# A two-layer perceiver block on one core: cross openings reordered, experts' up products split into fp32r passes

## The chip, the core and the metric

One Trainium2 chip, of which the program uses one core with its engines: TensorE (PE, with its weight loads PEld), VectorE (DVE), ScalarE (ACT), GpSimd (POOL) and the sync engine (SP), which here only issues DMAs. The metric is the time of one execution in device microseconds, lower is better. Before: median 1411.81 us of three runs, 1409.78 to 1412.41.

## The reference

The input x has 16 batches of 64 tokens and 256 features; it is 1024 x 256 as a matrix. Six sublayers each add to x what they compute from its layer norm:

```
x += cross0(norm(x), ctx, mask)          16 heads of 16, 1024 context rows per batch, softmax
x += self0(norm(x))                      attention over the batch axis, rotary, "softmax one"
x += moe(norm(x))                        8 experts, top 2, capacity 256, gelu(rows @ w1) @ w2
x += cross1(norm(x), ctx, bias, mask)    as cross0, with an additive bias row
x += self1(norm(x))                      attention over the sequence, rotary
x += fp4_linear(silu(gate) * up)         weights and activations rounded to a 4-bit grid in blocks of 16
```

For each batch a cross sublayer projects the 1024 x 256 context to keys and values, projects the queries, and forms softmax(q k / 4 + bias) v per head. In the experts, w1 is 256 x 1024 and w2 is 1024 x 256.

## The kernel before

**Cross block.** `cross_block` (line 192 on) runs all 16 batches in one block; batch b has eight steps n, one for each pair of heads. In a step TensorE computes the scores of pair n (`scores`, L476), transposes the probabilities of two steps before (`turn`, L489), and does one piece of the next batch's key or value projection (`project_key`, `project_value`, L419 to L421). In steps 5 and 1 it weighs the values of four pairs (`weigh`, L505). VectorE takes row maxima (L585), inverts the sums (L593), copies half of each transpose (L601) and computes the low part of the keys (`rest_key`, L573). ScalarE does the exponentials (L771), the other half of the copies (L780), the high part of keys (L755), the copies of values (L762) and the high part of the next context (`split_hi`, L747). GpSimd divides (L844), computes the context's low part (`split_lo`, L824) and spreads the queries into a block-diagonal operand (`spread`, L836). Each engine works through its own list in order and waits on semaphores; nothing is reordered at run time.

A projection is exact to fp32 by three fp32r passes: each operand is split into a rounded part hi and a rest lo, and the product is lo·hi + hi·lo + hi·hi:

```
pe.matmul(out, lhs[1], rhs[0], start=first, stop=False)
pe.matmul(out, lhs[0], rhs[1], start=False, stop=False)
return pe.matmul(out, lhs[0], rhs[0], start=False, stop=last)
```

**Opening.** Ahead of the loop over batches lies work for batch 0 and for all queries. TensorE computes batch 0's four key pieces (in the first cross block only the first of them, the other three behind the query products), transposes the first half of the normalized tokens (L520), projects their queries (`project_queries` 0 and 1, L530), computes batch 0's four value pieces, transposes the second half and projects its queries (2 and 3). VectorE splits each query product into hi and lo (`split_queries`, L668 to L672); the sync queue stores them to DRAM (`store_queries`, L336 and L337) and reloads them in the stacked layout (`first_queries`, L343); then `spread` can run, and then the first scores. The sync queue also copies the keys of each pair of heads into their stacked layout, three DMAs a pair (`load_keys`, L329). In the first cross block the queries of group 0 and 1 are stored first and the pairs 0 to 3 follow the reload of group 0, 4 to 7 that of group 1; in the second all eight pairs go ahead of the stores. Queries 2 and 3 are stored last, and ScalarE's first copy of batch 1's values (step 3) waits for those stores, since they lie in the same buffer. GpSimd does batch 1's four `split_lo` before `spread`.

The split of the context of batch b+2 is done in steps 1, 2, 5 and 6 of batch b (`SPLIT_STEPS`), and the load of context b+3 (L311) waits for its last piece, because all contexts come through one raw buffer.

**Experts.** `experts_block` (line 1470 on) does the eight experts one after the other: transposes of the gathered rows (L1516), the up product in eight f tiles of 128 hidden columns (L1530; fp32, two k steps, 256 columns), GELU on ScalarE (L1557), and the down product (L1540). VectorE copies the transposed rows (L1574) and the results (L1587), and in between rounds one chunk of the last sublayer's weights to the 4-bit grid (`Quantizer.run`, L1646 to L1655, ten passes). The sync queue loads up(e) when up product e-2 is done (L1496) and down(e) when down product e-2 is done (L1498). In expert 6 ScalarE and GpSimd also split the second cross block's weights and first context.

## Time and profile before

| what | value |
|---|---|
| median of three runs | 1411.81 us (1409.78 to 1412.41) |
| profiled execution, its own time | 1413.69 us |
| its span | 1411.9 us, 34686 instructions |
| TensorE busy | 1255.7 us (89%) |
| VectorE busy | 963.9 us (68%) |
| ScalarE busy | 760.5 us (54%) |
| GpSimd busy | 642.8 us (46%) |
| granted TensorE clock, mean | 0.926 of full |

Busy time is the time in which an engine works on an instruction; times are in us from the start of the span. The first cross block fills the span up to about 475 us, the experts lie between 626 and 752, the second cross block between 756 and about 1200. In a timeline row the bracket at the end is the idle time ahead of the instruction and what ended it, as far as the semaphores show it; `x4` means four such instructions in a row, merged. A fp32 product appears as two instructions, a fp32r pass as one.

### The profile page before, as it was taken

The numbers are of one execution on the slowest core, as the hardware profiler recorded it, in microseconds if no ns is written. First come the engines' busy times: TensorE is split into PE (matmuls) and PEld (weight loads), VectorE is DVE, ScalarE is ACT, GpSimd is POOL, SyncE is SP. The second block draws the span as 40 slices with busy tenths as digits, with TensorE's granted clock in tenths as the row PEclk, the third lists the DMA queues.
The fourth block names the chain that finished last, engine by engine and source line by source line (L and its number), as shares of the span: only waits on it lengthen the run. The fifth ranks groups of instructions, "written<-read, shape, count | busy, mean of one in ns | idle before, by whom it ended". The sixth has DMA issues, their size and how long they took to land. (4 is left out here: it accounts for less than half of the span.)

```text
span 1411.9 us, 34686 instructions
## 1 busy us (share of the span) xinstructions
PE 1255.7 (89%) x12166; PEld 1050.6 (74%) x12166; DVE 963.9 (68%) x1991; ACT 760.5 (54%) x1379; POOL 642.8 (46%) x580
## 2 busy tenths in 40 slices
PE   5799999999999689549997699999999998677778
PEld 3588888888887548338885588888888887546546
DVE  5477777777777565555515577777777777478896
ACT  2577777777786211102233577777777777124221
POOL 2465666665654314033341566656656654317000
PEclk9899999999999885559999899999999999886899
DMA  6677677777665140244545677777777765100000
GB/s 197 169 181 207 177 188 199 178 193 198 172 170 140 36 60 3 93 152 165 172 158 168 180 202 197 174 194 189 180 195 182 185 167 129 35 0 3 1 4 26
DMA packets 106723, 198.31 MB, mean 140 GB/s; under 512 B 43661, under 2 KB 63790, under 8 KB 106640
## 3 DMA queue, kind: packets, MB, share of 16 engines
q1 hardware_dynamic: 105104, 193.32, 52.0%
q0 software_dynamic: 1536, 3.88, 0.9%
q8 instruction: 53, 0.87, 0.3%
q14 instruction: 30, 0.25, 0.1%
HBM read 88.26 MB, written 10.62 MB: 70 GB/s over the span
## 5 line engine op out<-in xcount | busy, mean ns | idle before, releaser
L844 POOL TENSOR_SCALAR cross_prob<-cross_prob,cross_inverse 128x1024 f32<-128x1024 f32 x256 | 288.7, 1128 | 345.5 <-DVE cross_inverse L593 345.5
L771 ACT ACTIVATE cross_prob<-cross_negated,cross_negmax 128x1024 f32<-128x1024 f32 x256 | 294.9, 1152 | 147.9 <-DVE cross_negmax L585 147.5
L585 DVE CUSTOM_DVE_ANT_0 cross_negated<-cross_scores,cross_bias 128x1024 f32<-128x1024 f32 x256 | 313.5, 1225 | 31.1 <-PE cross_scores L476 13.7
L489 PE MATMUL cross_turn<-ident,cross_prob 128*128 128x128 f32 x2048 | 271.3, 275 | 16.2 <-POOL cross_prob L844 11.9
L489 PEld LDWEIGHTS cross_turn<-ident,cross_prob 128*128 128x128 f32 x2048 | 241.3, 142 | 55.9 <-POOL cross_prob L844 15.8
L780 ACT COPY cross_probT<-cross_turn 128x512 f32<-128x512 f32 x256 | 149.6, 584 | 69.2 <-PE cross_turn L489 68.2
L476 PE MATMUL cross_scores<-cross_keys,cross_qbd 96*128 96x512 f32 x512 | 169.6, 413 | 12.5 <-POOL cross_qbd L836 12.5
L601 DVE COPY cross_probT<-cross_turn 128x512 f32<-128x512 f32 x256 | 175.6, 686 | 5.4 <-PE cross_turn L489 5.4
L824 POOL TENSOR_TENSOR cross_ctx_lo<-cross_raw,cross_ctx_hi 128x512 fp32r<-128x512 f32 x120 | 156.2, 1303 | 25.7 <-ACT cross_ctx_hi L747 25.7
L419 PE MATMUL cross_out<-cross_wv_hi,cross_ctx_lo 128*128 128x256 f32 x488 | 147.4, 302 | 0.0
L421 PE MATMUL cross_out<-cross_wv_hi,cross_ctx_hi 128*128 128x256 f32 x488 | 137.4, 282 | 0.0
L420 PE MATMUL cross_out<-cross_wv_lo,cross_ctx_hi 128*128 128x256 f32 x488 | 137.2, 281 | 0.0
L593 DVE RECIPROCAL cross_inverse<-cross_total 128x1 f32<-128x1 f32 x256 | 41.9, 164 | 131.1 <-ACT cross_prob L771 129.9
L505 PE MATMUL cross_out<-cross_probT,cross_value 128*32 128x128 f32 x4096 | 127.2, 277 | 2.6 <-ACT cross_probT L780 1.8
L505 PEld LDWEIGHTS cross_out<-cross_probT,cross_value 128*32 128x32 f32 x4096 | 109.3, 111 | 26.0 <-issue 24.4
L419 PE MATMUL cross_proj<-cross_ctx_hi,cross_wk_lo 128*128 128x512 f32 x244 | 107.9, 442 | 0.0
L476 PEld LDWEIGHTS cross_scores<-cross_keys,cross_qbd 96*128 96x128 f32 x512 | 83.9, 191 | 32.2 <-POOL cross_qbd L836 14.1
L420 PE MATMUL cross_proj<-cross_ctx_lo,cross_wk_hi 128*128 128x512 f32 x244 | 97.5, 399 | 0.0
L421 PE MATMUL cross_proj<-cross_ctx_hi,cross_wk_hi 128*128 128x512 f32 x244 | 97.4, 399 | 0.0
L420 PEld LDWEIGHTS cross_out<-cross_wv_lo,cross_ctx_hi 128*128 128x128 f32 x488 | 92.8, 190 | 0.0
L573 DVE SCALAR_TENSOR_TENSOR cross_key_lo<-cross_proj,cross_bk,cross_key_hi 128x512 fp32r<-128x512 f32 x122 | 90.5, 742 | 3.3 <-ACT cross_key_hi L755 3.3
L419 PEld LDWEIGHTS cross_out<-cross_wv_hi,cross_ctx_lo 128*128 128x128 f32 x488 | 92.6, 190 | 0.0
(270 smaller groups left out, 2021.8 us busy)
## 6 DMA issues: line engine op xcount, KB each, us to landing
cross_keys<-cross_key_hi SPq DMA_DIRECT2D x512, 128.0 KB, 2.3
cross_raw<-in_ctxT SPq DMA_DIRECT2D x32, 1024.0 KB, 5.6
cross_keys<-cross_key_lo SPq DMA_DIRECT2D x256, 128.0 KB, 2.4
cross_bias<-bias_rows SPq DMA_DIRECT2D x32, 512.0 KB, 3.6
up_sb<-in_moe_w SPq DMA_DIRECT2D x8, 1024.0 KB, 9.1
down_sb<-in_moe_w SPq DMA_DIRECT2D x8, 1024.0 KB, 11.2
cross_stacked_q<-q_rows SPq DMA_DIRECT2D x90, 64.0 KB, 2.0
q_rows<-cross_negated SPq DMA_DIRECT2D x8, 256.0 KB, 2.5
```

The lines of the kernel that those rows point to most:

```text
L419: pe.matmul(out, lhs[1], rhs[0], start=first, stop=False)
L420: pe.matmul(out, lhs[0], rhs[1], start=False, stop=False)
L421: return pe.matmul(out, lhs[0], rhs[0], start=False, stop=last)
L476: last = pe.matmul(ps_s[n % 2][:, at], qbd[par][:, n, :, :].rearrange("p h q -> p (h q)"), keys[:, n, at], start=True, stop=True)
L489: last = pe.transpose(ps_t[part][:, k * P:(k + 1) * P], prob[n % 2][:, kt * P:(kt + 1) * P], ident)
L505: last = pe.matmul(ps_o[32 * j:32 * j + 32, 0:P], value[par][:, kt, g * P + 32 * j:g * P + 32 * j + 32], probT[:, j, kt, :], start=(kt == ...
L585: dve.tensor_tensor_reduce(negated[n % 2], ps_s[n % 2][:, :], bias_sb[par][:, :], -1.0, 3.0e38, ALU.add, ALU.min, negmax[:, n % 2:n % 2 + ...
L601: dve.tensor_copy(probT[:, j, 4:8, :], ps_t[1][:, :].rearrange("p (k q) -> p k q", k=4)).then_inc(turn_copied_v, 1)
L771: act.activation(prob[n % 2][:, :], negated[n % 2], ACT.Exp, bias=negmax[:, n % 2:n % 2 + 1], scale=-1.0, accum_out=total[:, n % 2:n % 2 + ...
L780: act.copy(probT[:, j, 0:4, :], ps_t[0][:, :].rearrange("p (k q) -> p k q", k=4)).then_inc(turn_copied_a, 1)
L824: pool.tensor_tensor(ctx_lo[par][:, :, at], raw[:, :, at], ctx_hi[par][:, :, at].bitcast(F32), ALU.subtract).then_inc(lo_done, 1)
L844: pool.tensor_scalar(prob[n % 2][:, :], prob[n % 2][:, :], inverse[:, n % 2:n % 2 + 1], 1.0, ALU.mult, ALU.mult).then_inc(prob_ready, 1)
```

## The change

**Cross openings.** On the sync queue keys and queries are interleaved: two pairs ahead in the first cross block (`taken is None`) and three in the second, then store of group 0, a pair, reload of group 0, store of group 1, a pair, reload of group 1. After the second context and batch 1's queries come the other pairs, with the stores of queries 2 and 3 between them, and the load of the output weights last. TensorE does all four key pieces ahead of the tokens in both blocks, and the query products 2 and 3 move into steps 0 and 1 of batch 0, behind the scores. Their splits on VectorE move to the same steps and get buffers of their own. In the second block VectorE's key rests and query splits move ahead of some of the additions of the experts' results. ScalarE splits context 1 ahead of the value copies. GpSimd, in the second block, spreads group 0 between the two halves of its context split. In batch 0 the context splits move from steps 1, 2, 5, 6 to 3, 4, 6, 7.

**Experts.** The up product uses three fp32r passes. ScalarE rounds the weights (four pieces) and the rows to their high part and takes over the copies of the results; VectorE computes the low parts. `up_hi`, `up_lo`, `rows_hi` and `rows_lo` are single buffers; the load of up(e) now waits only until the low part of expert e-2 is there. The norm's buffers are freed before the experts to make room. The weights' 4-bit rounding uses the class `Rounding` of the last sublayer: eight passes, of which the last comes behind the low parts. `Rounding` computes with negated scales; the sign of the silu input goes with it.

```diff
@@ cross_block, sync @@
-            def first_keys(g):
-                sp.wait_ge(key_lo_done, 2 * g + 2)
-                for n in range(4 * g, 4 * g + 4):
-                    load_keys(n)
+            def first_keys(n):
+                if n % 4 == 0:
+                    sp.wait_ge(key_lo_done, n // 2 + 2)
+                load_keys(n)
...
-            if taken is not None:
-                for g in range(G):
-                    first_keys(g)
-            for g in range(G):
-                store_queries(g, first_q_stored[g])
-            for g in range(G):
-                first_queries(g)
-                if taken is None:
-                    first_keys(g)
+            ahead = 2 if taken is None else 3
+            for n in range(ahead):
+                first_keys(n)
+            store_queries(0, first_q_stored[0])
+            first_keys(ahead)
+            first_queries(0)
+            store_queries(1, first_q_stored[1])
+            first_keys(ahead + 1)
+            first_queries(1)
             sp.wait_ge(lo_done, 8)
             load_ctx(2)
-            first.load_out(sp)
             sp.wait_ge(qbd_ready, G)
             load_queries(1)
-            for n in range(G, len(q_jobs)):
-                store_queries(n, q_stored)
+            for n in range(ahead + 2, 6):
+                first_keys(n)
+            store_queries(2, q_stored)
+            first_keys(6)
+            store_queries(3, q_stored)
+            first_keys(7)
+            first.load_out(sp)
@@ TensorE: four key pieces first; in body @@
                     scores(b, par, n)
+                    if is_first(b) and n < G:
+                        project_queries(G + n)
@@ VectorE, second block @@
-                for i in range(5, NT):
-                    through(i)
-                    rest_key(0, 0, i - 5)
-                shift(1)
-                rest_key(0, 0, 3)
-                for n in range(G):
-                    split_queries(n)
+                through(4)
+                through(5)
+                rest_key(0, 0, 2)
+                split_queries(0)
+                rest_key(0, 0, 3)
+                through(6)
+                through(7)
+                shift(1)
+                split_queries(1)
@@ ScalarE @@
+            copy_tokens(0)
+            for piece in range(4):
+                split_hi(1, 1, piece)
             for piece in range(4):
                 copy_value(0, 0, piece)
             copy_tokens(1)
-            for piece in range(4):
-                split_hi(1, 1, piece)
@@ GpSimd, second block @@
+                for piece in range(2):
+                    split_lo(1, 1, piece)
+                spread(0, 0, 0)
+                for piece in range(2, 4):
+                    split_lo(1, 1, piece)
+            spread(0, 0, 1)
@@ all @@
+        def split_steps(b):
+            return (3, 4, 6, 7) if is_first(b) else SPLIT_STEPS
@@ experts_block, sync @@
-                sp.wait_ge(hidden_ready, FT * (e - 1))
+                sp.wait_ge(up_divided, PIECES * (e - 1))
@@ TensorE @@
+                    pe.wait_ge(up_divided, PIECES * e + f * PIECES // FT + 1)
                     for g in range(G):
-                        last = pe.matmul(ps_h[f % 3][:, :], up[par][:, g, f * P:(f + 1) * P], rowsT[par][:, g, :],
-                                         start=(g == 0), stop=(g == G - 1))
+                        hi, lo = (part[:, g, f * P:(f + 1) * P] for part in (up_hi, up_lo))
+                        pe.matmul(ps_h[f % 3][:, :], lo, rows_hi[:, g, :], start=(g == 0), stop=False)
+                        pe.matmul(ps_h[f % 3][:, :], hi, rows_lo[:, g, :], start=False, stop=False)
+                        last = pe.matmul(ps_h[f % 3][:, :], hi, rows_hi[:, g, :], start=False, stop=(g == G - 1))
@@ ScalarE @@
+                if e + 1 < E:
+                    round_up(e + 1)
+                    round_rows(e + 1)
                 if e == E - 2:
                     first.round_weights(act)
+                for half in range(CT):
+                    copy_result(e, half)
+                if e == E - 2:
                     first.round_context(act)
@@ VectorE @@
+                    fp4.scale_and_round(dve, c, e)
                 if e + 1 < E:
-                    copy_turn(e + 1)
+                    rest_of_up(e + 1)
+                    rest_of_rows(e + 1)
```

`round_up(e)` is four ScalarE copies of 512 elements per partition into `up_hi`, `rest_of_up(e)` four VectorE subtractions into `up_lo`; `round_rows` and `rest_of_rows` do the same for the transposed rows in PSUM.

## Rows read from the trace of the kernel before

**Rows 1.** Windows, all engines: stretch, length, busy us, granted clock, DMA share.

```profile
70.00:460.00 390.00, 386.80 (x4160) 339.86 (x4154) 295.66 (x595) 298.79 (x528) 232.16 (x203) 1.00 0.71 181
58.50:64.00 5.50, 5.44 (x18) 4.58 (x19) 2.37 (x6) 4.46 (x8) 3.28 (x4) 0.50 0.17 65
628.20:638.20 10.00, 9.96 (x32) 8.25 (x33) 9.48 (x10) 2.69 (x7) 9.68 (x10) 0.69 0.11 28
645.58:652.49 6.91, 6.91 (x34) 6.03 (x33) 6.40 (x11) 2.69 (x7) 4.47 (x4) 1.00 0.61 205
```

**Rows 2.** Timeline, TensorE, opening of the first cross block: start, length, instruction.

```profile
37.52 1.03 PE L520 MATMUL cross_turn<-ident,cross_probT 128*128 128x128 f32 x8
...
46.50 1.49 PE L476 MATMUL cross_scores<-cross_keys,cross_qbd 96*128 96x512 f32 x4 [3.47 <-POOL cross_qbd L836]
...
58.56 1.94 PE L489 MATMUL cross_turn<-ident,cross_prob 128*128 128x128 f32 x8 [3.44 <-ACT cross_probT L780]
...
71.03 0.73 PE L476 MATMUL cross_scores<-cross_keys,cross_qbd 96*128 96x512 f32 x2
```

**Rows 3.** Timeline of the same opening, GpSimd and ScalarE.

```profile
39.87 5.58 POOL L824 TENSOR_TENSOR cross_ctx_lo<-cross_raw,cross_ctx_hi 128x512 fp32r<-128x512 f32 x4 [16.54 <-ACT cross_ctx_hi L747]
45.41 2.03 POOL L836 TENSOR_TENSOR cross_qbd<-cross_stacked_q,half_mask 96x512 fp32r<-96x512 f32 x2
...
56.74 0.62 ACT L747 CAST cross_ctx_hi<-cross_raw 128x512 fp32r<-128x512 f32 x1 [3.47 <-DMA cross_raw<-in_ctxT]
...
60.72 0.59 ACT L762 COPY cross_value<-cross_out 128x512 f32<-128x512 f32 x1 [0.66 <-DMA q_rows<-cross_value]
```

**Rows 4.** Timeline, TensorE, opening of the second cross block.

```profile
765.99 3.70 PE L530 MATMUL cross_scores<-cross_probT,cross_wq 128*128 128x512 f32 x8 [0.81 <-ACT cross_probT L787]
...
775.93 1.32 PE L520 MATMUL cross_turn<-ident,cross_probT 128*128 128x128 f32 x8 [0.51 <-DVE cross_probT L661]
...
790.64 2.07 PE L476 MATMUL cross_scores<-cross_keys,cross_qbd 96*128 96x512 f32 x4 [9.01 <-POOL cross_qbd L836]
...
809.61 0.73 PE L476 MATMUL cross_scores<-cross_keys,cross_qbd 96*128 96x512 f32 x2
```

**Rows 5.** Timeline of the same opening, sync queue, GpSimd and VectorE.

```profile
768.39 0.55 SPq L329 DMA_DIRECT2D cross_keys<-cross_key_hi  x1
...
770.95 1.01 POOL L851 TENSOR_TENSOR cross_rstd<-cross_shifted,cross_power 128x4 f32<-128x4 f32 x1 [7.69 <-DVE cross_shifted L655]
...
771.44 0.74 DVE L668 TENSOR_SCALAR cross_prob<-cross_scores,cross_bq 128x512 f32<-128x512 f32 x1
...
773.40 0.75 DVE L668 TENSOR_SCALAR cross_prob<-cross_scores,cross_bq 128x512 f32<-128x512 f32 x1
...
783.60 0.58 SPq L336 DMA_DIRECT2D q_rows<-cross_negated  x1
...
786.81 2.74 SPq L343 DMA_DIRECT2D cross_stacked_q<-q_rows  x6
...
789.55 1.04 POOL L836 TENSOR_TENSOR cross_qbd<-cross_stacked_q,half_mask 96x512 fp32r<-96x512 f32 x1 [5.50 <-DMA cross_stacked_q<-q_rows]
```

**Rows 6.** Timeline, TensorE, value products of the first opening, first and last of 48.

```profile
31.77 0.28 PE L419 MATMUL cross_scores<-cross_wv_hi,cross_ctx_lo 128*128 128x256 f32 x1
...
37.40 0.28 PE L421 MATMUL cross_out<-cross_wv_hi,cross_ctx_hi 128*128 128x256 f32 x1
```

**Rows 7.** Timeline, ScalarE and TensorE, second batch of the second cross block.

```profile
822.07 0.62 ACT L747 CAST cross_ctx_hi<-cross_raw 128x512 fp32r<-128x512 f32 x1 [0.16 <-DMA cross_raw<-in_ctxT]
...
823.98 0.59 ACT L780 COPY cross_probT<-cross_turn 128x512 f32<-128x512 f32 x1 [0.70 <-PE cross_turn L489]
...
826.04 1.04 PE L489 MATMUL cross_turn<-ident,cross_prob 128*128 128x128 f32 x8
```

**Rows 8.** DMA issues: tensors, engine, count, KB each, median us to landing.

```profile
down_sb<-in_moe_w SPq DMA_DIRECT2D x8, 1024.0 KB, 11.2
...
q_rows<-cross_value SPq DMA_DIRECT2D x8, 256.0 KB, 4.7
```

More of the change, by code:

```diff
@@ L549, in _ @@
             turn_tokens(1)
-            for n in range(G, 2 * G):
-                project_queries(n)
             def body(b, par):
@@ L686, in _ @@
             shift(0)
-            through(4)
+            if start is not None:
+                through(4)
+            else:
+                dve.wait_ge(rows_loaded, 48)
+                dve.wait_ge(q_loaded, 32)
+                rest_key(0, 0, 0)
+                rest_key(0, 0, 1)
             normalize(0)
@@ L694, in _ @@
                 dve.wait_ge(q_loaded, 32)
-                rest_key(0, 0, 0)
+                for piece in range(4):
+                    rest_key(0, 0, piece)
                 dve.wait_ge(rows_stored, 32)
@@ L1553, in _, with round_up, round_rows, copy_result @@
         def _(act):
+            def round_up(e):
+                if e >= 2:
+                    act.wait_ge(up_loaded[e % 2], 16 * (e // 2))
+                for p in range(PIECES):
+                    act.copy(up_hi[:, :, piece_of(p)], up[e % 2][:, :, piece_of(p)]).then_inc(up_rounded, 1)
+            def round_rows(e):
+                act.wait_ge(turned, e + 1)
+                act.copy(rows_hi[:, :, :], ps_t[:, :, :]).then_inc(rows_rounded, 1)
+            def copy_result(e, half):
+                act.wait_ge(result_ready, 2 * e + half + 1)
+                if half == 0 and e >= 2:
+                    act.wait_ge(scattered[e - 2], 16 * CT)
+                act.copy(result[e % 2][:, half, :], ps_y[half][:, :]).then_inc(result_copied, 1)
+            round_up(0)
+            round_rows(0)
             for e in range(E):
@@ L1744, in multiply, with __init__, part, scale_and_round @@
         return eng.tensor_tensor(self.by_block(out), self.by_block(self.v[:, at]), self.wide(self.scale, self.blocks_of(at)), ALU.mult)
+class GatedWeights:
+    ROWS = 2 * GU // P
+    TAILS = [(c, min(P, GU - c * P)) for c in range(-(-GU // P))]
+    ROW_CHUNKS = [(0, 3), (3, 6), (6, 9), (9, ROWS)]
+    def __init__(self, sb, gate_upT, downT):
+        self.gate_up, self.down = sb("gate_up_sb", [P, self.ROWS, D]), sb("down_sb", [P, G, GU])
+        self.gate_upT, self.downT = gate_upT, downT
+        self.q = Rounding(sb, "fp4w", 3 * D)
+        self.step, self.total = sb("fp4w_step", [P, 3 * D]), sb("fp4w_total", [P, 3 * D])
+    def part(self, chunk):
+        if chunk < len(self.ROW_CHUNKS):
+            first, end = self.ROW_CHUNKS[chunk]
+            return self.gate_up[:, first:end, :].rearrange("p r d -> p (r d)")
+        return self.down[:, chunk - len(self.ROW_CHUNKS), :]
+    def scale_and_round(self, dve, c, chunk):
+        x = self.part(chunk)
+        at = slice(0, x.shape[-1])
+        c.link(self.q.scales(dve, c, x, at))
+        c.link(self.q.divide(dve, x, at))
+        c.add(self.q.round(dve, c, self.step, self.total, at))
+    def multiply(self, dve, chunk):
+        x = self.part(chunk)
+        return self.q.multiply(dve, x, slice(0, x.shape[-1]))
+    def turn_row(self, pe, r, ps, ident):
+        for g in range(G):
+            last = pe.transpose(ps[:, g * P:(g + 1) * P], self.gate_up[:, r, g * P:(g + 1) * P], ident)
+        return last
+    def copy_row(self, act, r, ps):
+        return act.copy(self.gate_upT[:, :, r * P:(r + 1) * P], ps[:, :].rearrange("p (g n) -> p g n", g=G))
+    def turn_tail(self, pe, c, ps, ident):
+        m = self.TAILS[c][1]
+        for g in range(G):
+            last = pe.transpose(ps[0:m, g * P:(g + 1) * P], self.down[:, g, c * P:c * P + m], ident)
+        return last
+    def copy_tail(self, act, c, ps):
+        m = self.TAILS[c][1]
+        return act.copy(self.downT[0:m, c, :], ps[0:m, :])
 class Ahead:
```

171 lines of the change are left out of this document (56 added, 115 removed).

## The prediction

> **What bounds the kernel now.** I read the stretches first. In the middle of a cross block TensorE is busy for 386.8 of 390.0 us at granted clock 1.00, and in an expert's up stage for 6.91 of 6.91 us [rows 1]. So time is bought in two ways only: fewer TensorE cycles in the experts, or removing the idle time at the two openings, where TensorE has nothing. The timeline of the openings shows that idle time. In opening 1 the last token transposes end at 38.5, four query products follow, and the first scores start at 46.50, held by the spreading on GpSimd [rows 2]. GpSimd had spread late because four context subtractions of 5.58 us stand before the spreading, and they started at 39.87 [rows 3]. Two ScalarE waits follow, for the third context (56.74, 3.47 us) and for the stored queries (60.72, 0.66 us) [rows 3], and TensorE stands still for 3.44 us and goes on at 0.50 of its clock [rows 1, 2]. In opening 2 the first scores wait until 790.64, 9.01 us idle [rows 4]: all 24 key transfers are issued first (768.39 on), the queries are stored only at 783.60 and reloaded at 786.81, and the spreading starts at 789.55 [rows 5]. In the experts TensorE never waits, so every us of product there is one of the end.
>
> **Part 1, the experts' up products.** Each expert had 32 fp32 instructions of 256 columns in 6.91 us [rows 1], 0.216 each. Now there are 8 x 2 x 3 = 48 fp32r passes of the same shape, 128 x 128 weights and 256 columns. The opening's value products are exactly that: 48 passes from 31.77 to 37.40, (37.40 - 31.77) / 47 = 0.120 apart [rows 6]. 48 x 0.120 = 5.75, so 1.16 us less; experts 1 to 7 give 8.1. Bounds: 0.107 a pass if only the columns count (half of the 0.216 that a two-fold fp32 instruction takes), 12.1 us in all; above, 0.190, about the length of a weight load (6.03 us by 33 loads is 0.183) [rows 1], under the rivals. I take 0.120, the same form.
> The Trainium skill, "TensorE: Matmul & The Clock Gate", Part 3, says that a weight load overlaps a running matmul only when the row group differs. By it load and stream would add to about 0.30 a pass and the experts would become some 60 us slower; rows 6 speak against it, since 0.120 is below one load.
> Expert 0's up product filled 628.2 to 638.2 at a mean clock of 0.69 [rows 1]; between the levels 0.50 and 1.00 that is half speed for 0.31 / 0.50 x 10 = 6.2 us, until 634.4. Its token rows now go through a ScalarE cast and then a VectorE subtraction instead of one copy: about 0.74 more (a 512-element VectorE pass of rows 5), start 629.0. At half the clock an f tile of 6 passes takes 6 x 0.213 = 1.28 (twice the column time), so 4.2 tiles until 634.4, then 3.8 x 0.72 = 2.7: end at 637.1 against 638.2, gain 1.1.
> The work around it: ScalarE gets four casts (about 0.62 each [rows 7]), one row cast and two result copies per expert, VectorE four subtractions and one (3.7). They start when the last f tile is done and run under the down product, 6.9 us long by the same instruction count. The chain of casts and subtractions needs about 0.5 + 4 x 0.62 + 0.7 + 0.74 = 4.4 of 7.3, so 2.9 us of cover remain. VectorE's fp4 rounding has two passes fewer and its last multiply stands behind the subtractions: hidden. One place isn't: in expert 6 the order on ScalarE is weights, two result copies, context casts, and the second result is ready only at the end of the down product. The context casts (four, 2.2 us with their overlap) then stand ahead of expert 7's first GELU by 1.8 us, and with three banks TensorE stalls for about 1.0 (0 if they hide, 2.2 if nothing does). The loads: down(e) and then up(e+1) are now issued together, at the end of a down product; a down load takes 11.2 us to landing [rows 8], an up load is of the same size, so both are there after 11.2 to 22.4. The first cast of up(e+1) is due after 5.75 + 0.43 + 6.9 + 5.75 + 0.5 = 19.3, with 2.9 of cover: 0.2 us late at the very worst, which I cost at 0. The Trainium skill, "DMA: Bandwidth & Descriptors", gives about 2 us and bytes over 436 GB/s, an estimate of 4.4 us for 1 MB, also no wait; the row here is more than twice that.
> Sum of part 1: 8.1 + 1.1 - 1.0 = 8.2.
>
> **Part 2, opening 1.** TensorE now does all key products before the tokens. Piece 0 starts at 14.4, pieces 1 to 3 wait for the fourth context subtraction (17.9); with passes of 512 columns at 0.43 (four times 0.107) at half speed, and about 0.23 once the clock has risen, which I put at 21.8, they end at 23.9 (0.43 throughout: 25.6). Tokens 1.0, copies 1.1, two query products 3.7 (the same instructions as in [rows 4]): end 29.7. This is 2 us later than before, and two VectorE splits of 1.96 each [rows 5] end at 31.85. Store, reload and spread then take what opening 2 shows: two stores issued in 1.0, the reload at most 2.1 behind them, three reload issues 1.4, landing 1.4 behind [rows 5]. The interleaved transfer of pair 2 (1.9) fills the wait for the store. Group 0: store 29.9, pair 2 until 32.8, reload until 34.3, landed 35.7, spread until 36.8. ScalarE's four casts come now directly behind the first token copies (26.0 to 28.2), and GpSimd's 5.58 us end at 32.3, so they no longer stand in the way. TensorE's value products (5.75 from 29.7) and second transposes end at 36.7. First scores at 36.8 against 46.50: 9.7 earlier. What is late next is the ScalarE copy of the next batch's first value in step 3. It waits for the second queries' stores, which the sync queue issues behind: reload of group 1 (until 38.7), context 2, the wait for the second spreading (41.1), the next queries (1.6), pairs 4 and 5 (3.8), one store, pair 6 (1.9), the other store. That is 50.2, landed 52.0. ScalarE would be there at 47.8: a wait of 4.2 us, so the exponential of step 3 starts at 53.2 (61.7 before). From there: turn 2 at 53, scores 5 at 56, product of group 0 at 59.5, scores of step 6 at 61.4 against 71.03 [rows 2], gain 9.6. The added query products (1.9 each) in steps 0 and 1 and their splits are in these times; before, they stood ahead of the loop in TensorE's idle time.
> Two costs: the clock may fall in the new wait, as it did behind 3.44 us of idle time [rows 2]; half speed costs an instruction its own time again, I take 0.9 (0 to 2.7, half of the 5.5 us stretch of rows 1). And the split of context 2 ends in step 7 instead of 6, so context 3 is fetched 2.9 us later. In the second cross block that cast had waited 0.16 for its transfer, and the transpose two steps on stood at 826.04 with its copy started at 823.98 [rows 7]; 2.9 late with about 2.2 of slack costs 0.7 (0 to 2.9).
> Part 2: 9.6 - 0.9 - 0.7 = 8.0.
>
> **Part 3, opening 2.** TensorE's order stays, VectorE's changes: the first two key rests at 762.0, so that pairs 0 to 2 leave at 763.5 (5.7 us of issues; eight pairs took 15.2 from 768.39 to 783.60 [rows 5]), group 0 is split at 769.9 and stored, pair 3, reload at 773.0, landed 776.5 at latest. GpSimd's second root now ends at 774.7 (3 us later than the row, since two additions moved behind the split), two context subtractions 2.8: 777.5, spread until 778.5. The transposes of rows 4 end at 777.3, so the scores start at 778.6 against 790.64: 12.0 earlier. The second group: split 775.5, reload until 780.2, spread 783.3; then as in part 2 to the last store, issued until 790.4, landed 792.3. ScalarE would be there at 789.2; wait 3.5. Exponential of step 3 at 793.9, 8.2 later the scores of step 6: 802.1 against 809.61 [rows 4], 7.5. Less 0.5 for the clock and 0.7 for context 3: 6.3.
>
> The other edits (silu without a scale, the buffers' places, the output weights' load moved behind the keys) move no instruction that anything waits for: 0.
> **Sum:** 8.2 + 8.0 + 6.3 = 22.5. The profiled execution took 1413.69 for a span of 1411.9; 1413.7 - 22.5 = 1391.2 there. It lay 1.9 above the median of 1411.81, so the forecast is 1411.8 - 22.5 = 1389.3 us. Against a change of 0.2% (2.8 us), what a measurement of this kernel can tell from none, this is large.
>
> **Rivals.**
> A, the stores become the gate of both openings. A store of second queries took 4.7 us to landing [rows 8], and here context 2's 1 MB is in the queues with it. 2.5 to 4 us later in each opening, with the half clock for longer: 1389.3 + 7 = 1396. For it: the 0.66 us of rows 3, where this wait already showed. Against: in opening 2 the reload followed a store within 2.1.
> B, the new wait is covered: ScalarE runs ahead of TensorE, and if stores land before ScalarE comes, 3 us of each opening and the half clock come back, 1389.3 - 7 = 1382. For it: pairs issued early free the queues. Against: the count of 14 issues ahead of the last store.
> C, slower: the up passes are paced by the weight load, 0.190, because each pass changes weights and the per-tile waits stop the pulling ahead. 48 x 0.190 = 9.12, 2.2 more than before, 17.7 for eight experts. 1411.8 + 17.7 - 14.3 = 1415.2. It decides from 0.181 a pass on, where an up stage costs 6.91 + 14.3 / 8 = 8.7. Against it stand rows 6.
> D, the openings don't gain at all, since later work catches up on the same transfers: 1411.8 - 8.2 = 1403.6. Against: TensorE is busy for 99% afterwards [rows 1], so an earlier start can't be absorbed.
>
> **Chances.** Forecast 0.68, A 0.14, B 0.11, D 0.04, C 0.03. The range: the likeliest one's unknown costs (clock 0 to 2.7, context 3 0 to 2.9, expert 7 0 to 2.2) give 1385 to 1394; with most of A and B 1382 to 1397. Faster by over 0.2%: 0.96; within 0.2%: 0.02; slower: 0.02 (C's time lies just over 0.2%).
>
> **What would show it.** Up products in 5.75 us with 48 passes 0.120 apart; TensorE idle of about 1 us in expert 7's up stage behind a GELU; first scores 9.7 and 12.0 us earlier, counted from the block's start; a ScalarE wait for the query stores of 3.5 to 4.2 us in step 3 of both first batches; a wait for the context in step 1 of the second batch near 3 us. The prediction is wrong if passes are over 0.15 apart, if the scores wait for spreading beyond 40, or if a load of expert weights appears as a wait.

## The result, and the profile after

Changed kernel: median 1399.93 us of 8 runs (1398.30 to 1403.66); kernel before, on the same chip: 1411.01 of 8 (1407.66 to 1414.08). The ratio is 0.9925, 95% interval 0.9913 to 0.9938: faster by 11.1 us. The forecast was 22.5 us faster, and its range ended at 1397. In the profiled executions the span went from 1411.9 to 1399.4, 12.5 us. Cut at points that both traces have, this is where the time went (us; a minus is time gained):

| stretch | before | after | change | forecast |
|---|---|---|---|---|
| start to first weighing of values, cross 1 | 69.15 | 62.77 | -6.4 | -8.7 |
| first to fifth weighing | 52.40 | 54.40 | +2.0 | +0.7 |
| fifth weighing to routing table | 495.07 | 494.99 | -0.1 | 0 |
| routing table to experts' first turn | 9.73 | 13.14 | +3.4 | 0 |
| first turn to cross 2's first key product | 130.34 | 120.96 | -9.4 | -8.2 |
| first key product to first weighing, cross 2 | 51.04 | 46.17 | -4.9 | -7.0 |
| first to fifth weighing | 52.38 | 54.21 | +1.8 | +0.7 |
| fifth weighing to the end | 551.79 | 552.76 | +1.0 | 0 |

Opening 1, TensorE's timeline (start, duration, engine and line, operation, out<-in; in brackets the idle time ahead and its releaser). L483 are scores, L496 turns, L512 the weighing. The two score rows answer to [rows 2].

```profile
37.84 0.74 PE L483 MATMUL cross_scores<-cross_keys,cross_qbd 96*128 96x512 f32 x2 [1.70 <-POOL cross_qbd L837]
...
56.02 1.89 PE L496 MATMUL cross_turn<-ident,cross_prob 128*128 128x128 f32 x8 [4.48 <-ACT cross_probT L785]
...
64.65 0.73 PE L483 MATMUL cross_scores<-cross_keys,cross_qbd 96*128 96x512 f32 x2
```

The scores start 8.7 us earlier than before, but only 6.4 are left at step 6 (71.03 in [rows 2]): TensorE stood still for 4.48 us, as predicted in place and longer in size, and its granted clock was 0.51 from 56.0 to 59.4. Who held it shows in ScalarE's timeline and the sync queue's: the last of the four store issues (two halves for each group), and the copy that waits for them.

```profile
54.80 0.58 ACT L767 COPY cross_value<-cross_out 128x512 f32<-128x512 f32 x1 [5.42 <-DMA q_rows<-cross_value]
...
79.57 0.62 ACT L752 CAST cross_ctx_hi<-cross_raw 128x512 fp32r<-128x512 f32 x1 [2.62 <-DMA cross_raw<-in_ctxT]
...
107.02 0.62 ACT L752 CAST cross_ctx_hi<-cross_raw 128x512 fp32r<-128x512 f32 x1 [2.95 <-DMA cross_raw<-in_ctxT]
```
```profile
39.61 0.43 SPq L314 DMA_DIRECT2D cross_raw<-in_ctxT  x1
...
47.73 0.58 SPq L339 DMA_DIRECT2D q_rows<-cross_value  x1
...
51.35 0.44 SPq L340 DMA_DIRECT2D q_rows<-cross_value  x1
...
73.74 0.39 SPq L314 DMA_DIRECT2D cross_raw<-in_ctxT  x1
```

The store issued until 51.8 was there at 54.8, 3.0 us later. The waits for a context at 79.57 and at 107.02 are the 2.0 us between the first and the fifth weighing; the forecast had only the first of them.

The experts' start, TensorE (L1530 turns, L1544 to L1546 the three passes) and GpSimd's and the sync queue's issues:

```profile
625.30 1.11 PE L1530 MATMUL experts_t<-ident,experts_rows 128*128 128x128 f32 x4 [9.54 <-DMA experts_rows<-stored_rows,gather_at]
...
627.82 0.58 PE L1544 MATMUL experts_h<-experts_rows_hi,experts_up_lo 128*128 128x256 f32 x1 [1.40 <-DVE experts_rows_lo L1621]
...
643.38 0.28 PE L1545 MATMUL experts_h<-experts_rows_lo,experts_up_hi 128*128 128x256 f32 x1
...
648.89 0.28 PE L1546 MATMUL experts_h<-experts_rows_hi,experts_up_hi 128*128 128x256 f32 x1
```
```profile
617.54 1.66 POOL L1643 DMA_INDIRECT experts_rows<-stored_rows,gather_at  x1 [30.24 <-POOLq L1357]
...
619.51 1.25 POOL L1643 DMA_INDIRECT experts_rows<-stored_rows,gather_at  x1 [0.30 <-issue]
```
```profile
619.96 0.37 SPq L1510 DMA_DIRECT2D up_sb<-in_moe_w  x1
```

Expert 1's passes from 643.38 to 648.89 are the second to the last of 48: 5.51 / 46 = 0.120 apart, the forecast's pace. But the first turn stands idle for 9.54 us ahead of it; in the kernel before it was 6.12 (626.35). Expert 2's 1 MB of up weights is now issued at 619.96, in the middle of the gathers; before it left at 638.43. The second gather, issued at 619.51, landed at 625.26.

Opening 2, VectorE's timeline (L670 to L674 split the second group, L663 normalizes the second half) and TensorE's:

```profile
765.70 1.74 DVE L674 TENSOR_TENSOR cross_negated<-cross_prob,cross_negated 128x512 fp32r<-128x512 f32 x1
767.47 5.36 DVE L663 TENSOR_SCALAR cross_probT<-x,cross_moments,cross_rstd 128x256 f32<-128x256 f32 x4
```
```profile
746.26 0.77 PE L426 MATMUL cross_scores<-cross_ctx_hi,cross_wk_lo 128*128 128x512 f32 x1 [3.25 <-PEq L2057]
...
756.62 3.70 PE L537 MATMUL cross_scores<-cross_probT,cross_wq 128*128 128x512 f32 x8 [0.87 <-ACT cross_probT L792]
...
768.85 0.41 PE L527 MATMUL cross_turn<-ident,cross_probT 128*128 128x128 f32 x2 [2.79 <-DVE cross_probT L663]
...
772.25 1.54 PE L527 MATMUL cross_turn<-ident,cross_probT 128*128 128x128 f32 x6 [2.98 <-DVE cross_probT L663]
...
773.44 1.20 PE L483 MATMUL cross_scores<-cross_keys,cross_qbd 96*128 96x512 f32 x2
```
```profile
765.62 2.93 POOL L825 TENSOR_TENSOR cross_ctx_lo<-cross_raw,cross_ctx_hi 128x512 fp32r<-128x512 f32 x2
768.52 1.08 POOL L837 TENSOR_TENSOR cross_qbd<-cross_stacked_q,half_mask 96x512 fp32r<-96x512 f32 x1
769.56 2.48 POOL L825 TENSOR_TENSOR cross_ctx_lo<-cross_raw,cross_ctx_hi 128x512 fp32r<-128x512 f32 x2
```

Four normalizations took 5.36 us. The same four took 1.38 in the first half of this opening and in the kernel before. One by one they took 1.23, 3.56, 0.40 and 0.40: the first beside a context subtraction, the second (768.63 to 772.19) while GpSimd went through the spreading and two subtractions, the last two with GpSimd idle. TensorE waited twice for the tokens. So the scores came 27.2 us behind the block's first key product instead of the forecast's 22.1 (778.6 less 756.5), which is 6.8 earlier than in the kernel before (33.95) and not 12.0.

One more us went ahead of that. The query products (756.62) start 10.4 us behind the first key product; in the kernel before it was 9.3 (765.99 in [rows 4] less 756.69). The granted clock was 0.50 for the first 6.1 us of the key products, against 3.9 before.

### The profile page after: what moved, and what is told of

The parts are those of the page before. It is cut to its first block and busy times, and to the rows that moved or that the text cites. A ratio compares the mean times of both kernels' runs of the same rounds, so it can differ in the third digit from the quotient of the medians.

```text
span 1399.4 us, 35051 instructions
## 1 busy us (share of the span) xinstructions
PE 1249.0 (89%) x12294; PEld 1050.5 (75%) x12294; DVE 974.2 (70%) x1995; ACT 784.7 (56%) x1435; POOL 636.1 (45%) x580
## 5 line engine op out<-in xcount | busy, mean ns | idle before, releaser
L496 PE MATMUL cross_turn<-ident,cross_prob 128*128 128x128 f32 x2048 | 273.0, 276 | 16.3 <-POOL cross_prob L845 8.9
L496 PEld LDWEIGHTS cross_turn<-ident,cross_prob 128*128 128x128 f32 x2048 | 241.7, 142 | 57.2 <-POOL cross_prob L845 13.0
L483 PE MATMUL cross_scores<-cross_keys,cross_qbd 96*128 96x512 f32 x512 | 170.4, 414 | 1.7 <-POOL cross_qbd L837 1.7
L825 POOL TENSOR_TENSOR cross_ctx_lo<-cross_raw,cross_ctx_hi 128x512 fp32r<-128x512 f32 x120 | 155.8, 1300 | 10.2 <-ACT cross_ctx_hi L752 10.2
L512 PE MATMUL cross_out<-cross_probT,cross_value 128*32 128x128 f32 x4096 | 128.3, 278 | 1.6 <-ACT cross_probT L785 1.2
L512 PEld LDWEIGHTS cross_out<-cross_probT,cross_value 128*32 128x32 f32 x4096 | 110.4, 112 | 25.1 <-issue 23.9
L483 PEld LDWEIGHTS cross_scores<-cross_keys,cross_qbd 96*128 96x128 f32 x512 | 83.4, 190 | 21.0 <-issue 13.8
L428 PEld LDWEIGHTS cross_out<-cross_wv_hi,cross_ctx_hi 128*128 128x128 f32 x488 | 92.9, 190 | 0.0
```

Source lines behind the costliest of these rows:

```text
L483: last = pe.matmul(ps_s[n % 2][:, at], qbd[par][:, n, :, :].rearrange("p h q -> p (h q)"), keys[:, n, at], start=True, stop=True)
L496: last = pe.transpose(ps_t[part][:, k * P:(k + 1) * P], prob[n % 2][:, kt * P:(kt + 1) * P], ident)
L512: last = pe.matmul(ps_o[32 * j:32 * j + 32, 0:P], value[par][:, kt, g * P + 32 * j:g * P + 32 * j + 32], probT[:, j, kt, :], start=(kt == ...
L825: pool.tensor_tensor(ctx_lo[par][:, :, at], raw[:, :, at], ctx_hi[par][:, :, at].bitcast(F32), ALU.subtract).then_inc(lo_done, 1)
```

## The experiments

Each is compared with runs of the kernel before on the same chip (medians 1410.2 to 1410.6). There is no number 7. The intervals reach 2 to 3 us to either side, so besides the ratio I read each trace by the stretches of the table above. Each kernel has one trace, and the same code differs from trace to trace: opening 1 by 2.2 us (the changed kernel and experiment 3), and in the kernels with the change the stretch from the fifth weighing to the routing table from 493.8 to 497.0 and the one from the fifth weighing of cross 2 to the end from 550.1 to 553.2. "Opening 1" is the time of the first weighing, "contexts" the stretch from the first to the fifth weighing (52.4 in the kernel before), "opening 2" first key product to first weighing.

```
kernel                       median   ratio to before, 95%    opening1 contexts table-turn experts opening2 contexts
before                                                         69.2     52.4      9.7      130.3   51.0     52.4
changed                     1399.93  0.9925 [.9913,.9938]      62.8     54.4     13.1      121.0   46.2     54.2
1 experts alone             1405.96  0.9962 [.9947,.9977]      68.9     52.4     13.2      120.6   51.8     52.4
2 openings alone            1406.45  0.9966 [.9950,.9982]      63.7     54.7      9.7      130.3   46.9     53.4
3 up load late              1398.30  0.9917 [.9897,.9938]      65.0     54.8     10.4      120.6   45.9     53.6
4 subtractions behind norm  1401.51  0.9932 [.9911,.9953]      63.3     54.6     13.2      120.4   48.6     53.9
5 split steps as before     1395.52  0.9891 [.9874,.9908]      64.7     52.4     13.1      119.9   46.0     52.4
6 stores ahead              1395.15  0.9895 [.9879,.9912]      59.5     53.5     13.0      120.4   45.7     53.8
8 own home                  1393.95  0.9883 [.9864,.9901]      58.5     53.8     13.0      121.1   45.7     53.8
9 all mends                 1386.07  0.9826 [.9811,.9842]      58.2     53.7     10.4      120.1   42.0     52.4
10 all but 4's              1386.37  0.9843 [.9821,.9865]      57.0     52.4     10.4      120.6   45.9     52.4
11 all, steps as before     1383.93  0.9810 [.9793,.9827]      59.1     52.4     10.4      120.7   42.3     52.4
12 all, and behind queries  1382.59  0.9808 [.9792,.9823]      56.4     52.4     10.5      120.0   42.3     52.4
```

**1 and 2, the two parts alone.** The kernel before with the hunks of the experts, and with those of the cross block.

> The kernel before with the change to the experts alone. The changed kernel's trace gives the expert stage 130.2 -> 120.8 us, a gain of 9.4, and a loss of 3.4 at the first gathered rows, because the load of expert 2's up weights (1 MB) is now issued beside the gathers. Theory 1 (the loss belongs to the experts part): the span falls by 9.4 - 3.4 - 0.5 for the clock = 5.5, about 1405.5 us, and the first turn of the experts comes about 3.4 later behind the routing table than before. Theory 2 (the loss comes from the openings' earlier clock or transfers): 9.4, about 1401.6, and the first turn stands 6.1 us of idle time behind the table, as before. The prediction on record said 8.2: 1402.8.

> The kernel before with the change to the two openings alone, the experts in fp32. From the changed kernel's trace: lead of 4.6 us at the end of the first cross block, 4.9 from opening 2, 1.8 lost again at the third context of opening 2, 0.5 at the last turns: 7.2, about 1403.8 us. Theory 1 (the parts add up): 1403 to 1405, and the first gathered rows are there 6.1 us behind the table. Theory 2 (the parts disturb one another, as by the clock): opening 2 gains the 6.3 that were predicted and the sum is 10 or more, 1401 or less.

The ratios stand for 5.4 and 4.8 us, together 10.2, where the changed kernel's stands for 10.6; the spans fell by 4.8 and 7.2, together 12.0 of 12.5. Within their intervals the parts add up. The later gathered rows belong to the experts' part: 13.2 us behind the table with it, 9.7 without. Opening 2 gained 4.2 us with the cross part alone (51.0 to 46.9), so what it falls short of is its own; theory 2 there is wrong. The median of experiment 2 (1406.45) lies outside theory 1's 1403 to 1405; its profiled span fits (1411.9 less 7.2 is 1404.7).

**3, the load that met the gathers.**

```
+            sp.wait_ge(turned, 1)
             for e in range(2, E):
```

> The changed kernel, but the load of expert 2's up weights waits for the first turn of the experts (one wait more on the sync queue; it is due about 20 us later). Theory 1 (the 1 MB load holds up the gathered rows): the idle time ahead of the first turn falls from 9.5 to about 6.8 us and the end comes 2.7 earlier, about 1397.2. Of the 3.4 us, 0.7 stay, since the first two gathers take 1.66 and 1.25 us to issue instead of 1.21 and 0.96, beside VectorE's subtractions. Theory 2 (the longer issue is the whole cause, and the landing only follows it): no change within 0.5 us, 1399.9. If later loads of weights become late, it is slower: a wait on PE or ACT in expert 2 would show it.

TensorE's first turn in that kernel:

```profile
624.53 1.11 PE L1531 MATMUL experts_t<-ident,experts_rows 128*128 128x128 f32 x4 [6.81 <-DMA experts_rows<-stored_rows,gather_at]
```

6.81 us of idle time, as theory 1 has it to the tenth, and no wait in expert 2 (the experts' stretch stays at 120.6). The two issues still took 1.66 and 1.25 us, which leaves the other 0.7. The medians (1398.30 against 1399.93) don't show it, since the intervals overlap; this opening 1 happened to be 2.2 us longer.

**4, GpSimd's subtractions behind the normalization in opening 2.**

```
             else:
-                for piece in range(2):
+                spread(0, 0, 0)
+                pool.wait_ge(normed, NT)
+                for piece in range(4):
                     split_lo(1, 1, piece)
-                spread(0, 0, 0)
-                for piece in range(2, 4):
-                    split_lo(1, 1, piece)
-            spread(0, 0, 1)
+                spread(0, 0, 1)
```

> The changed kernel with GpSimd in another order in opening 2: spreading of group 0, then a wait until VectorE has normalized the second half, then the four context subtractions, then the spreading of group 1. (In opening 1 both spreadings stand behind the subtractions, as before in effect.) In the changed kernel's trace the four normalizations took 5.36 us beside the subtractions and 1.38 us in the kernel before, and TensorE stood still for 2.79 and 2.98 us in its last transposes. Theory 1 (the two engines hold each other up): they take 1.38 us again, the first scores come 3.5 to 4 us earlier, and the end by 3 to 4 us, about 1396.4. Theory 2 (they were slow for another reason, as their source in memory): still above 4 us and no gain, 1399.9. Rival of theory 1: the later subtractions hold the spreading of group 1 and the third context, and under 1 us is left.

Both the theory and its rival came true, in turn. VectorE, TensorE and ScalarE of that kernel:

```profile
766.90 2.19 DVE L663 TENSOR_SCALAR cross_probT<-x,cross_moments,cross_rstd 128x256 f32<-128x256 f32 x4
```
```profile
769.33 1.00 PE L483 MATMUL cross_scores<-cross_keys,cross_qbd 96*128 96x512 f32 x2
...
788.01 1.94 PE L496 MATMUL cross_turn<-ident,cross_prob 128*128 128x128 f32 x8 [3.75 <-ACT cross_probT L785]
```
```profile
786.80 0.59 ACT L767 COPY cross_value<-cross_out 128x512 f32<-128x512 f32 x1 [4.70 <-DMA q_rows<-cross_value]
```

The normalization takes 2.19 us (its first instruction, beside the spreading, took 1.22, the others 0.40 each), and the scores start 22.3 us behind the first key product, 4.9 earlier. All of it is lost at the next gate: group 1 is spread only behind the subtractions, the sync queue waits for that, the last store leaves at 782.9 and is there at 786.8. The first weighing is 2.4 us later than in the changed kernel.

**5, the split's steps.** `return SPLIT_STEPS` in place of the first batch's (3, 4, 6, 7).

> The changed kernel with one constant put back: in the first batch the context's split stands in steps 1, 2, 5, 6 again instead of 3, 4, 6, 7. Theory 1 (the late last piece holds the next context's load, and that its own cast two and three groups later): context 3 is fetched 2.7 us earlier, the ScalarE waits for a context in the second and third batch (2.6 and 2.9 us in the first block, 3.7 in the second) fall under 0.5, and the interval from the first to the fifth weighing of values falls from 54.4 to 52.4 us in the first block and from 54.2 to 52.4 in the second: 3.8 us in all, about 1396. Theory 2 (context 3 waits for the queues, not for its issue): the waits stay within 1 us of what they were and the time at 1399.9. A loss is possible in the first batch, where the cast of step 1 can wait for context 2; in the changed kernel the stored queries end that wait later anyway.

Theory 1: the contexts' stretches are 52.4 in both blocks, 3.8 us less than in the changed kernel, and the median is 4.4 lower. The profiled execution was the slowest of the four (1400.56): its opening 1 is 1.9 us and its stretch up to the routing table 2.0 us longer than in the changed kernel's trace. The cast in step 1 cost nothing that shows, since ScalarE waits for the stores afterwards (4.32 us there).

**6 and 8, the stores.** In 6 stores 2 and 3 are issued ahead of key pairs 4 to 7 in opening 1. In 8 the second queries' halves lie elsewhere, so that no copy waits for their store:

```
-q_home = [..., first.value1[:, :, :].rearrange("p t d -> p (t d)")]
+q_home = [..., oT[:, :, :].rearrange("p g t -> p (g t)")]
...
-                if isinstance(b, int) and b == 1 and piece == 0:
-                    act.wait_ge(q_stored, 32 * (len(q_jobs) - G))
```

> The changed kernel with another order on the sync queue: the third and the fourth store of queries stand ahead of key pairs 4 to 7 (in opening 2 pair 5 stays between them). In opening 1 the last store then leaves at about 47.7 instead of 51.8. Theory 1 (the ScalarE wait of 5.4 us in step 3 is set by the order of issue): it falls by 4 to about 1.5 us and the first weighing comes 4 us earlier, about 1396. Theory 2 (it is set by how long a store takes beside the 1 MB of context 2, as 4.4 us in opening 2 of the experiment before): the wait ends at 51.5 to 52.5 and 2 to 3 us are gained, about 1397.5. No change at all would mean that another wait stood behind it.

> The changed kernel with the second queries' halves in another buffer (oT, free at that time), so that ScalarE's copy of the next batch's values needs no stored queries; the wait moves to VectorE's first result, in step 6. Theory 1 (this wait is the whole of what opening 1 fell short): the wait of 5.4 us is gone, TensorE doesn't stand still for 4.5 us and keeps its clock, and the first weighing comes 5 to 6 us earlier in opening 1 and 0.5 in opening 2: about 1394. Theory 2 (a wait for the context, 1 MB, takes its place in the same step, since its cast stands two places behind): a wait for DMA of 1 to 4 us at the cast in step 3, and 2 us gained, about 1398.

In 6 the wait is down to 0.50 us and the first weighing comes at 59.5, 3.3 earlier. In 8, theory 1, it comes at 58.5, though its first scores were 1.5 later (39.32 against 37.84). From the first scores to the first weighing it is 19.1 us instead of 24.9, so the wait and the half clock behind it were 5.8 of opening 1. The granted clock stayed at 1.00 there (52.8 to 57.0). ScalarE passes the place of the wait without one, and TensorE stays busy:

```profile
51.22 0.56 ACT L767 COPY cross_value<-cross_out 128x512 f32<-128x512 f32 x1
```
```profile
52.85 0.63 PE L483 MATMUL cross_scores<-cross_keys,cross_qbd 96*128 96x512 f32 x2
53.32 1.04 PE L496 MATMUL cross_turn<-ident,cross_prob 128*128 128x128 f32 x8
```

**9, all mends; 10, the same without experiment 4's order.** (9 has the split in steps 2, 3, 5, 6.)

> All mends together: the queries' own home, the load of expert 2's up weights behind the first turn, GpSimd's subtractions of opening 2 behind the normalization, the context's split of the first batch in steps 2, 3, 5, 6. By the ledger: 2.7 (gathers) + 5.5 (opening 1) + 4 (opening 2, where the earlier scores can now count) + 3.8 (contexts) = 16, about 1384. If the openings end at a context transfer instead, half of 9.5 is left: 1388 to 1390. Not below the changed kernel by 6 or more: the ledger is wrong.

> The kernel with all mends, but GpSimd's order in opening 2 as in the changed kernel (two context subtractions, spreading, two more, spreading), so beside the normalization. Theory 1 (VectorE and GpSimd hold each other up, and this counts once the stored queries no longer gate the opening): the four normalizations take 5.4 us again instead of 2.20, TensorE's idle time in the last transposes goes from 0.92 + 0.64 back to 2.8 + 3.0, and the time from the block's first key product to the first weighing of values in opening 2 grows from 41.95 to about 45.5: about 1389.5. Theory 2 (the 3.7 us between the two kernels at that place came from the context's split steps or the own home): under 1 us, 1386 to 1387.

9 is 13.9 us below the changed kernel's median, 16 expected. 10 shows that experiment 4's order was right, with the gate behind it gone: opening 2 is 42.0 us with it and 45.9 without, and the normalization takes 5.36 us again. The medians of the two (1386.07, 1386.37) don't show these 3.9 us: opening 1 came 1.3 later and the contexts took 1.4 more in 9's profile, both at the same code, and such differences between traces are as large as the effect.

**11 and 12.** 11 is 9 with the split in steps 1, 2, 5, 6. In 12 GpSimd waits in opening 1 for `q_step` 3 ahead of its subtractions.

> The kernel with all mends and the context's split of the first batch in steps 1, 2, 5, 6 instead of 2, 3, 5, 6. In the kernel with all mends a wait of 1.4 us for context 3 and one of 2.8 us for context 4 are left in the first cross block. Theory 1 (they stem from the shifted first pieces): both fall under 0.5 and 1 us comes back, 1385. Theory 2 (they stem from the transfer's own time behind an issue that the last piece, step 6 in both, fixes): they stay, and the early cast in step 1 waits for context 2 on ScalarE: 0 to 2 us slower, 1386 to 1388.

> The kernel with all mends, and in opening 1 GpSimd's four context subtractions wait until VectorE has split the first group of queries. There VectorE's last step took 1.67 us beside them and takes 0.69 alone. Theory 1 (the two hold each other up, and the first scores hang on this split): that step takes 0.69 us, the first query store leaves about 1.0 earlier behind the query product, and the first weighing comes 0.5 to 1.0 earlier: about 1385.3. Theory 2: the second group's split and the normalization are held up in its place (2.1 and up to 5.4 us instead of 1.38), and the second transposes come later than the spreading: slower by 1 to 3 us, about 1388.

11: no wait for a context above 0.9 us is left, and both stretches are as in the kernel before. Theory 1 holds for the wait for context 3 only: it is 1.4 us in 9, 1.6 in 10 and 1.4 in 12, all with steps 2, 3, 5, 6, and gone in 11. The 2.8 us for context 4 are in 9 alone (0.7 in 10, 0.6 in 12), so the steps didn't make them. And 10 and 12 have 52.4 us in both stretches as well: the shifted steps cost no time that these traces show, and the intervals of 9 and 11 overlap. 12, theory 1 on VectorE's row:

```profile
30.07 0.69 DVE L674 TENSOR_TENSOR cross_negated<-cross_prob,cross_negated 128x512 fp32r<-128x512 f32 x1
...
32.51 1.67 DVE L674 TENSOR_TENSOR cross_negated<-cross_prob,cross_negated 128x512 fp32r<-128x512 f32 x1
```

The step takes 0.69 us alone, and the second group's has the 1.67 in its place. The first store of queries is issued 2.0 us after the split begins, and 3.0 in 9, 10 and the changed kernel. From there to the first weighing little of it is left: the weighing comes 27.6 us after the split begins, against 28.0 in 10 and 30.1 in 9, which have the same code in this opening. The 0.4 us against 10 are less than the two traces of the same code differ by, so theory 1's gain isn't shown beyond the store. The median of 1382.59 us is the lowest here, 27.6 below the kernel before; its interval overlaps with 11's.

## Why the prediction was wrong

The mechanisms named were there; the sum failed by 10.0 us of span. Five terms were too good: the gathers by 3.4, opening 1 by 2.3, opening 2 by 2.1, the contexts by 2.4 and the end by 1.0. The experts gave 1.2 more than forecast.

**Part 1, right in size, with a missed place.** "Both are there after 11.2 to 22.4 ... which I cost at 0" looked at whom the loads serve and not at whom they meet. The load of expert 2 was moved by the new wait (`up_divided` of expert 0, done at 619.9) to the gathers of the first rows: 3.4 us lost, of which experiment 3 gives 2.7 back. In the openings the prediction followed each DMA of a moved step, and here it didn't. The other 0.7: the gathers' issue takes 1.66 and 1.25 us beside VectorE's subtractions of the up weights, 1.21 and 0.96 without them (experiment 2). The stage itself went as worked out: first turn to last down product 111.65 to 103.20, 8.4 against 8.2 (13.09 a period instead of 14.25; expert 7's stall 0.68 instead of 1.0). Another 0.9 came behind the last down product, where I had looked for nothing: luck.

**Part 2, the store.** The step "that is 50.2, landed 52.0" was 51.8 and 54.8. The landing of 1.8 had no row of its own; the row of 4.7 us [rows 8] stood in rival A. Here the store ran beside key pairs (context 2 had landed at 45.0, before the first of these stores was issued at 47.73) and took 3.0. The first scores were 1.0 late, and with the half clock the first weighing came at 62.8 instead of 60.4: 2.3 us. The 1.0 is the failure of part 3 in another place. "GpSimd's 5.58 us end at 32.3, so they no longer stand in the way" put them beside VectorE's split of group 0. It began on time (27.91) and took 3.0 us instead of 1.96, its last step 1.67 instead of 0.69, and the store left at 30.94 instead of 29.9. Of rival A (1396, 0.14) the mechanism was there in opening 1, by 1.2 us of landing and not by its 2.5 to 4. In opening 2 the four halves landed 2.1 to 2.7 us behind their issue, and there it was not. Experiments 6 and 8 show that the wait for the stores was the gate of opening 1.

**Part 3, two engines side by side.** "two context subtractions 2.8: 777.5 ... The transposes of rows 4 end at 777.3" put GpSimd's work beside VectorE's as if it were free. It made the normalization 5.36 us and the split 1.74. Nothing of this was in the sum, though the kernel before has it: a split that takes 0.69 alone took 1.63 beside GpSimd's subtractions. That cost 3.9 (9 against 10; 0.4 of it is the clock at the key products, below), of which some was hidden in the changed kernel, since ScalarE then waited only 0.49 us for the stores instead of the 3.5 predicted: 2.1 us short in all. The two waits stand one behind the other, so removing the first alone gave nothing (experiment 4).

Another part of the late scores is not GpSimd's. In every kernel with the changed order on GpSimd (the changed one and 2, 3, 5, 6, 8, 10) the first scores of opening 2 start 16.8 us behind the query products, and in 4, 9, 11 and 12 it is 12.2 to 12.3. But the query products start 9.1 to 10.4 us behind the first key product, and they follow how long the granted clock stays at half there (3.1 us in 8, 6.1 in the changed kernel). The forecast kept the 9.3 of the kernel before; the changed kernel had 10.4, 1.1 of the 5.1 us by which its scores were late. Why the clock stayed at half for longer is open.

Beside one GpSimd instruction a normalization took 1.1 to 1.4 us, about as long as the instruction (1.03 to 1.75), and one took 3.56 through three of them in a row, in all seven kernels with the changed order on GpSimd. The Trainium skill, "SBUF — State Buffer", section "SBUF: two separate sides", says that GpSimd and VectorE share a port pair as an exclusive lock. A GpSimd instruction takes it, or a VectorE one in a two-port mode or with two inputs in SBUF against a GpSimd read of SBUF; the first to start holds it for its whole length, and the other is blocked. The trace agrees in kind, by 5.36 against 1.38; in which mode VectorE ran it doesn't say. That one instruction is blocked through three of the other engine's is shown by the 3.56 us alone. The same section says that GpSimd can't write a DMA's descriptors while VectorE runs in a two-port mode. Here the issue of a gather took 1.66 against 1.21 us beside VectorE's subtractions, which have two inputs in SBUF; for those the section names the lock and not the descriptors, and no experiment takes the subtractions away. I had not weighed this page.

**The context's echo.** The prediction charged the late last piece once, 0.7 in each opening. A late split also makes the next load late: in block 1 the stretch grew by 2.0 us through two waits, in block 2 by 1.8. Experiment 5 gives all of it back with one constant.

**The last 1.0** lies in the last 41 us of cross 2 (its 1161.06 to 1202.20, before 1174.55 to 1214.69), where the granted clock was 0.88 against 0.96 before. Most of it is from the last weighing to the output product: 5.6 us against 4.8 before. That piece is 4.2 in experiment 3 and 5.9 in 2, 4, 5, 8 and 12, and the whole stretch behind the fifth weighing runs from 550.1 to 553.2 in the kernels with the change. So the 1.0 isn't shown to belong to the change; where the scatter comes from is open.

One reading of the rows was wrong without a cost: behind the transposes at 37.52 two query products follow (39.33 to 43.0), not four.

Rivals C and D are refuted by 0.120 us a pass and by the openings' ratio of 0.9966 alone. B, the covered wait, held in opening 2 only, for a bad reason: the scores were late themselves. The measured 1399.93 lies outside A's time too: the gathers and the two engines side by side were in no rival.

## What to carry to other kernels

When a wait is changed, ask of every transfer behind it what else is in flight at its new time, not only when its data are due. Work moved beside other work is free only if the two engines don't slow each other: look in the trace for the same instruction alone and beside the other. When one wait is removed, look at once for the next on the same path, and price it with the slow landing, not the quiet one; a mend that shows nothing (experiment 4) can be worth 4 us once the second gate is gone. And before a small difference is put down to an edit, look for a kernel with the same code at that place.

## What was unexpected of the hardware

- A VectorE normalization of 128x256 fp32 from SBUF to SBUF took 0.41 us alone (four in a row 1.38), 1.1 to 1.4 beside one GpSimd instruction and 3.56 through three in a row; the subtraction of 512 columns with two inputs in SBUF 0.69 and 1.63 to 1.74. An instruction that reads PSUM (0.75 us) was not slower there.
- The issue of the first two gathers on GpSimd took 1.66 and 1.25 us beside VectorE's subtractions, 1.21 and 0.96 without; the second landed 5.75 us behind its issue when a 1 MB load was issued 0.45 us after it, and 3.02 without (experiment 3).
- A 256 KB half of a query store landed 2.1 to 3.4 us behind its issue in the changed kernel. With a context's 1 MB still in flight it took 4.3 to 5.0 (experiment 4, opening 2, the two halves issued up to 779.4) and 4.9 to 5.8 (kernel before, opening 1).
- fp32r passes with a weight load of 0.190 us each still went 0.120 apart, in the experts as in the openings.
